# Moving the four query-norm matmuls behind the last attention-value matmuls of each head

## The chip, the cores and the metric

The kernel runs on the 8 cores of one Trainium2 chip. Every core runs the same program on its own batch element (there are 8), and the cores exchange nothing. The metric is the device time of the slowest core in microseconds (us).

## The reference

One transformer layer with its normalizations around each half, per batch element, sequence 2048, width 2048, 16 heads of 128:

```python
# x: [8, 2048, 2048] f32
h   = layernorm(x)
q   = einsum('bpd,hde->bphe', h, W_Q) + b_Q        # k and v likewise
s   = einsum('bqhe,bkhe->bhqk', q, k) / sqrt(128)
s   = where(causal, s, -1e5)
z   = einsum('bkhe,bhqk->bqhe', v, softmax(s))
x   = x + layernorm(einsum('bqhe,hed->bqd', z, W_O) + b_O)
bw  = where(w >= 0, 1, -1) * mean(abs(w), axis=1, keepdims=True)
x   = x + layernorm(einsum('bsi,oi->bso', layernorm(x), bw) + bias)
```

## The kernel before

The program is written as one list of instructions for each engine. `Plan.op` appends an instruction to its engine's list together with the semaphore values that it waits for, so the order of the calls in the Python code is the order on each engine. Nothing reorders them later. Waits are separate small instructions on line 45, one for each semaphore, and each increments or is compared with one counter per engine (PE, DV for VectorE, SC for ScalarE, GP for GpSimd).

Stage A (to about 190 us in the profile) normalizes x, transposes it into `arena_a` (bf16, 16 chunks of 128 features by 2048 positions), and computes q, k and v of head 0 on the way.

Then come the 16 heads, one after the other. For head h, in the order of the code from line 524 on:

- `emit_w_mms(h, 1)` and `emit_w_mms(h, 2)` (line 316) make k and v: 64 matmuls each (line 362), 16 chunks by 4 slices of 512 positions, into four PSUM banks. For k these banks are psD, psE and the two halves of psC; for q and v they are the halves of psA and psB. Four VectorE instructions (line 376) add the bias and write `qt`, `kt`, or v's staging area in `ptil`.
- `emit_mh_sq(which, h)` (line 453) squares q (which = 0) or k (which = 1) with one VectorE instruction of 128x2048 (line 460) into `sqb`, a part of the tile that the profile calls `c`.
- `emit_mh_mms(which, h)` (line 463) multiplies these squares by a matrix of ones: 4 matmuls (line 473) into psA and psB, so that every position's squared norm stands in each row. Each is followed by a VectorE maximum over one row (line 479), and at the end come a maximum of the four (line 485) and a logarithm on ScalarE (line 490). From the norms of q and k comes one number per head, an upper bound of the scores that the exponentials subtract.
- v is transposed (line 554) and copied (line 560). Then four groups g = 0 to 3 of 512 queries follow. Each computes scores (line 572), exponentials on ScalarE (line 586), causal masks on GpSimd (lines 609 and 612), column sums by matmuls with ones (line 622), their reciprocals on ScalarE (lines 627 and 631), the scaling of the probabilities on VectorE (line 641, one instruction for each chunk of 128 keys), the products with v (line 660, 4, 8, 12 and 16 matmuls into psE; called the AV matmuls here), the copy of psE to a staging tile (line 676), and a store to memory (line 679).

PE runs something else while ScalarE and VectorE make the scaled probabilities. In groups 0 to 2 that is the first scores of the next group. In group 3, with no next group, it is the q projection of the next head: lines 650 to 653. This is the place of the change, passed 15 times (after heads 0 to 14), and called a head boundary below:

```python
elif h + 1 < H:
    emit_w_mms(h + 1, 0)      # 64 matmuls, 4 bias adds
    emit_mh_sq(0, h + 1)      # square of q
    emit_mh_mms(0, h + 1)     # 4 matmuls, 5 maxima, 1 logarithm
pe_av = 0
for j in range(chunks):       # 16 AV matmuls in group 3
    wait = [("DV", dv_norm[j])]
```

After the AV matmuls follow the copy of psE (line 676), and then on PE the k projection of head h + 1. Its first matmul writes psD; its waits include the copy of psE, because its second matmul writes psE (lines 339 to 344).

After the heads, the sign weights of the second half are made and transposed (from line 401 on), and 16 row tiles go through the output projection, two normalizations and the second matrix product (lines 718 to 897).

Of the kernel before, what the change touches and what calls it, by code (L numbers as in the profile page):

```python
# [60 lines left out]
def build_program(SEQ, DM, H):  # L61
# [8 lines left out]
    NG = NT // TPG  # L70
# [382 lines left out]
    def emit_mh_sq(which, h):  # L453
        src = (qt_sb, kt_sb)[which]
        if which == 0:
            w0 = [("DV", dv_qkv_evac_d[(h, 0)]), ("PE", pe_mb_prev),
                  ("PE", pe_bw_last), ("PE", pe_norm_last)]
        else:
            w0 = [("DV", dv_qkv_evac_d[(h, 1)]), ("PE", pe_norm_last)]
        dv_sq_d[which] = p.op("vector", lambda e, s=src: e.tensor_mul(  # L460
            sqb, s[:], s[:]), wait=w0, inc="DV")

    def emit_mh_mms(which, h):
        nonlocal pe_norm_last, dv_red_last, sc_lns
        for s in range(NSL):
            hb = s % 4
            wait = [("DV", dv_sq_d[which]), ("CONST", const_t),
                    ("SC", psbuf_last_rd[hb])]
            if which == 1:
                wait.append(("DV", dv_red_d[(0, s)]))  # L470
            if s == 0 and (which == 1 or h == 0):
                wait.append(("DV", dv_qkv_evac_d[(h, 2)]))
            pe_norm_last = p.op("tensor", lambda e, s=s, hb=hb: e.matmul(  # L473
                [psA[:, 0:SLW], psA[:, 512:512 + SLW], psB[:, 0:SLW],
                 psB[:, 512:512 + SLW]][hb], onem_sb[:],
                sqb[:, s * SLW:(s + 1) * SLW], start=True, stop=True),
                wait=wait, inc="PE")
            dv_red_d[(which, s)] = p.op(
                "vector", lambda e, s=s, hb=hb, wh=which: e.reduce_max(
                    srow[0:1, wh * 8 + s:wh * 8 + s + 1],  # L480
                    [psA[0:1, 0:SLW], psA[0:1, 512:512 + SLW],
                     psB[0:1, 0:SLW], psB[0:1, 512:512 + SLW]][hb], AX.X),
                wait=[("PE", pe_norm_last)], inc="DV")
        p.drain("vector")
        dv_mx_d[which] = p.op("vector", lambda e, wh=which: e.reduce_max(  # L485
            srow[0:1, 16 + wh:17 + wh], srow[0:1, wh * 8:wh * 8 + NSL],
            AX.X), inc="DV")
        dv_red_last = dv_mx_d[which]
        p.drain("scalar")
        t_ln = p.op("scalar", lambda e, wh=which: e.activation(  # L490
            srow[0:1, 18 + wh:19 + wh], srow[0:1, 16 + wh:17 + wh], AF.Ln,
            bias=0.0, scale=1.0), wait=[("DV", dv_mx_d[which])],
            inc="SC" if which == 1 else None)
        if which == 1:
            sc_lns = t_ln
# [28 lines left out]
    for h in range(H):  # L524
# [40 lines left out]
        def emit_score(g, j, pe_sc):  # L565
            hb = j % 4
            wait = [("SC", psbuf_last_rd[hb])]
            if j == 0:
                wait += [("DV", dv_vch[h]), ("DV", dv_qkv_all)]
                if g == 0:  # L570
                    wait.append(("DV", dv_mx_d[1]))
            pe_sc[j] = p.op("tensor", lambda e, j=j, g=g, hb=hb: e.matmul(  # L572
                schalf[hb], kt_sb[:, j * 128:(j + 1) * 128],
                qt_sb[:, g * GQ:(g + 1) * GQ], start=True, stop=True),
                wait=wait, inc="PE")
# [27 lines left out]
        for g in range(NG):  # L603
            chunks = (g + 1) * TPG
            gp_mask_j = {}
            for r in range(TPG):
                j = g * TPG + r
                if r > 0:
                    p.op("gpsimd", lambda e, j=j, r=r: e.memset(  # L609
                        ptil[:, j * GQ:j * GQ + r * 128], 0.0),  # L610
                        wait=[("SC", sc_exp[j])], inc="GP")
                gp_mask_j[j] = p.op("gpsimd", lambda e, j=j, r=r: e.tensor_tensor(  # L612
                    ptil[:, j * GQ + r * 128:j * GQ + (r + 1) * 128],
                    ptil[:, j * GQ + r * 128:j * GQ + (r + 1) * 128],
                    tri_sb[:], ALU.mult), wait=[("SC", sc_exp[j])], inc="GP")
            pe_den = 0
            for j in range(chunks):
                wait = [("SC", sc_exp[j])] if j < g * TPG else \
                    [("GP", gp_mask_j[j])]
                if j == 0:  # L620
                    wait.append(("SC", sc_rinv_prev))
                pe_den = p.op("tensor", lambda e, j=j, chunks=chunks: e.matmul(  # L622
                    psC[:, 512:512 + GQ], onem_sb[:], pslot[j],
                    start=(j == 0), stop=(j == chunks - 1)),
                    wait=wait, inc="PE" if j == chunks - 1 else None)
            p.drain("scalar")
            p.op("scalar", lambda e: e.activation(
                psC[:, 512:512 + GQ], psC[:, 512:512 + GQ], AF.Ln,
                bias=0.0, scale=1.0), wait=[("PE", pe_den)])
            p.drain("scalar")  # L630
            sc_rinv = p.op("scalar", lambda e, g=g: e.activation(  # L631
                rbc[g % 2], psC[:, 512:512 + GQ], AF.Exp, bias=0.0, scale=-1.0),
                wait=[("DV", rbc_war[g % 2])], inc="SC",
                lowp="softmax normalizer becomes a bf16 matmul operand")
            sc_rinv_prev = sc_rinv
            dv_norm = {}
            for j in range(chunks):
                wait = [("SC", sc_rinv)] if j == 0 else []
                if j == 0:
                    wait.append(("PE", pe_den))  # L640
                dv_norm[j] = p.op("vector", lambda e, j=j, g=g: e.tensor_tensor(  # L641
                    pslot[j], pslot[j], rbc[g % 2], ALU.mult),
                    wait=wait, inc="DV")
            rbc_war[g % 2] = dv_norm[chunks - 1]
            nchunks = (g + 2) * TPG
            if g + 1 < NG:
                pe_sc = {}
                for j in range(min(4, nchunks)):
                    emit_score(g + 1, j, pe_sc)
            elif h + 1 < H:  # L650
                emit_w_mms(h + 1, 0)
                emit_mh_sq(0, h + 1)
                emit_mh_mms(0, h + 1)
            pe_av = 0
            for j in range(chunks):
                wait = [("DV", dv_norm[j])]
                if j == 0:
                    wait += [("DV", dv_zevac.get(gidx - 1, 0)),
                             ("DV", max(dv_bw_evac_half))]
                pe_av = p.op("tensor", lambda e, j=j, chunks=chunks: e.matmul(  # L660
                    psE[:, 0:GQ], v_sb[:, j * 128:(j + 1) * 128], pslot[j],
                    start=(j == 0), stop=(j == chunks - 1)),
                    wait=wait, inc="PE")
                ptil_slot_av[j] = pe_av
            pe_av_all[h] = pe_av
            if g + 1 < NG:
                sc_exp = {}
                for j0 in range(0, min(4, nchunks), estep):
                    emit_exp(g + 1, j0, pe_sc, sc_exp)
                for j in range(min(4, nchunks), nchunks):  # L670
                    emit_score(g + 1, j, pe_sc)
                    if (j + 1) % estep == 0 and j + 1 > 4:
                        emit_exp(g + 1, j + 1 - estep, pe_sc, sc_exp)
            zpar = gidx % 2
            wait = [("PE", pe_av), (ZWs[zpar], zw_par_t[zpar])]
            dv_zevac[gidx] = p.op("vector", lambda e, zpar=zpar: e.tensor_copy(  # L676
                zstage[zpar], psE[:, 0:GQ]), wait=wait, inc="DV")
            zw_par_t[zpar] = p.op(
                "sync", lambda e, g=g, h=h, zpar=zpar: e.dma_start(
                    zs_h.ap()[g * TPG:(g + 1) * TPG, h].transpose([1, 0, 2]),  # L680
                    zstage[zpar].rearrange("p (t q) -> p t q", q=128)),
                wait=[("DV", dv_zevac[gidx])], inc=ZWs[zpar], incn=16)
            gidx += 1

    B_PE = p.cnt("PE")
    B_DV = p.cnt("DV")
# [253 lines left out]
def _get_nc():  # L940
    key = (_SEQ, _DM, _H)
    if key not in _nc_cache:
        _nc_cache[key] = build_program(*key)
    return _nc_cache[key]
# [30 lines left out]
```

How the kernel before makes its waits and increments, by code:

```python
        def thunk(e, fn=fn, wait=wait, inc=inc, incn=incn, lowp=lowp):  # L43
            for (s, v) in wait:
                e.wait_ge(sems[s][0], v)
            if lowp is not None:
                with nc.allow_low_precision(reason=lowp):
                    ins = fn(e)
            else:
                ins = fn(e)
            if inc is not None:
                ins.then_inc(sems[inc][0], incn)
```

## Time and profile before

| | us |
|---|---|
| runs shown | 2677.37 and 2810.69, median 2744.03 |
| profiled execution, its own time | 2676.51 |
| profiled execution, span of the slowest core (core 7) | 2674.3 |
| spans of the 8 cores | 2662.7 to 2674.3 |
| heads 0 to 15 (about) | 190 to 1855 |
| PE busy on core 7 | 1928.7 (72%) |
| VectorE busy | 992.5 (37%) |
| ScalarE busy | 554.6 (21%) |

The profiled execution is one run, and its rows are those of core 7. A row of the timeline gives the start, the length, the engine, the line of the kernel, output<-input, the shape, and how many instructions stand together; in brackets is how long the engine had been idle before and what released it. A matmul's own length overlaps the next one's, so the distance of starts is what a matmul in a row costs. PE is TensorE, PEld its weight loads, DVE VectorE, ACT ScalarE, POOL GpSimd. PEclk is TensorE's granted clock as a share of full speed, 1.00 being 2.4 GHz and 0.50 being 1.2 GHz.

### The profile page before, as it was taken

Reading aid. Unit: us, or ns where it says so; the run is one execution under the profiler, and the core shown is the slowest. Engines: PE = TensorE matmul, PEld = TensorE weight load, DVE = VectorE, ACT = ScalarE, POOL = GpSimd, SP = SyncE. Lnnn points to the kernel's source line nnn. Section 1 sums busy time; section 2 is a strip of 40 time slices with the busy share of each in tenths; the row PEclk is TensorE's granted clock in tenths of the full one; section 3 lists DMA queues with packets and bytes.
Section 4 is the critical chain, followed back from the end, with each engine's and each line's share of the span. In section 5 each row is a group of like instructions: output and inputs, shape, how many; then the busy total and the mean of one; then the engine's idle time right before and its main releaser. Section 6 shows DMA issues by size and latency. Waiting matters only on the chain.

```text
span 2674.3 us, 27043 instructions; the slowest of 8 cores (2662.7 to 2674.3 us)
## 1 busy us (share of the span) xinstructions
PE 1928.7 (72%) x8180; PEld 827.8 (31%) x8336; DVE 992.5 (37%) x1760; ACT 554.6 (21%) x737; POOL 240.0 (9%) x558
## 2 busy tenths in 40 slices
PE   1457787787777877878778778775438877878874
PEld 1322332332323323323233233232223333333331
DVE  3533333332332232333323333334673435344343
ACT  1223213123032131230321312303001111111110
POOL 1001101011011010110111111201000000000000
PEclk9679898898998988988989889898657988988886
DMA  6322121121221211112113232323322122122110
GB/s 151 110 40 24 12 28 14 20 22 16 25 24 13 28 14 20 22 14 26 22 14 39 35 51 22 46 34 103 112 95 60 53 65 79 40 79 77 42 56 31
DMA packets 178474, 119.32 MB, mean 45 GB/s; under 512 B 168100, under 2 KB 168100, under 8 KB 170148
## 3 DMA queue, kind: packets, MB, share of 16 engines
q0 software_dynamic: 107200, 75.51, 16.8%
q1 hardware_dynamic: 71140, 42.07, 6.3%
q8 instruction: 78, 1.28, 0.2%
q14 instruction: 56, 0.46, 0.1%
HBM read 125.97 MB, written 25.17 MB: 57 GB/s over the span
## 4 chain that ended last, share of the span: by engine, by line
PE 53%; DVE 17%; ACT 10%; issue 9%; DVEq 5%; POOL 3%; DMA 2%; ACTq 1%; POOLq 0%; another core or an unknown queue 0%
PE psA L362 8%; PE psB L362 8%; PE psE L660 7%; ACT ptil L586 5%; PE psC L847 5%; PE psC L362 4%; DVEq L58 4%; PE psC L622 3%; DVE st L210 3%; PE psE L847 2%; PE psD L847 2%; POOL ptil L612 2%; PE psD L362 2%; PE psE L362 2%; DMA c<-x 2%
## 5 line engine op out<-in xcount | busy, mean ns | idle before, releaser
L641 DVE TENSOR_TENSOR ptil<-ptil,c 128x512 bf16<-128x512 bf16 x640 | 220.4, 419 | 482.2 <-ACT c L631 445.4
L362 PE MATMUL psA<-arena_a,wbuf 128*128 128x512 bf16 x1002 | 298.3, 383 | 6.7 <-ACT arena_a L276 3.8
L362 PE MATMUL psB<-arena_a,wbuf 128*128 128x512 bf16 x1002 | 296.5, 380 | 4.9 <-ACT arena_a L276 3.8
L660 PE MATMUL psE<-ptil,v 128*128 128x512 bf16 x625 | 205.4, 428 | 55.8 <-DVE ptil L641 54.7
L622 PE MATMUL psC<-ptil,onem_sb 128*128 128x512 bf16 x624 | 181.6, 403 | 54.0 <-POOL ptil L609 25.0
L586 ACT ACTIVATE ptil<-psA,mbias 128x1024 bf16<-128x1024 f32 x160 | 178.3, 1114 | 183.5 <-PE psE L660 78.4
L847 PE MATMUL psC<-arena_a,c 128*128 128x512 bf16 x496 | 165.8, 416 | 59.5 <-DVE c L834 58.7
L490 ACT ACTIVATE srow<-srow 1x1 f32<-1x1 f32 x32 | 6.5, 202 | 913.6 <-DVE srow L485 913.6
L612 POOL TENSOR_TENSOR ptil<-ptil,tri_sb 128x128 bf16<-128x128 bf16 x256 | 109.2, 426 | 896.2 <-ACT ptil L586 896.1
L586 ACT ACTIVATE ptil<-psB,mbias 128x1024 bf16<-128x1024 f32 x160 | 177.1, 1107 | 0.2 <-PE psB L572 0.2
L572 PE MATMUL psA<-qt,kt 128*128 128x512 bf16 x314 | 107.5, 425 | 81.7 <-ACT ptil L586 51.2
L362 PE MATMUL psC<-arena_a,wbuf 128*128 128x512 bf16 x538 | 155.9, 379 | 4.9 <-DVE qt L376 4.5
L210 DVE BATCH_NORM_STATS2 st<-wbuf 128x6 f32<-128x512 f32 x64 | 39.6, 681 | 317.5 <-ACT wbuf L870 317.5
L362 PEld LDWEIGHTS psA<-arena_a,wbuf 128*128 128x128 bf16 x1024 | 100.8, 99 | 130.0 <-issue 14.3
L362 PEld LDWEIGHTS psB<-arena_a,wbuf 128*128 128x128 bf16 x1024 | 100.3, 98 | 124.0 <-issue 5.6
L660 PEld LDWEIGHTS psE<-ptil,v 128*128 128x128 bf16 x640 | 68.3, 107 | 205.8 <-issue 184.3
L572 PE MATMUL psB<-qt,kt 128*128 128x512 bf16 x315 | 107.9, 427 | 26.1 <-ACT ptil L586 25.7
L473 PE MATMUL psA<-c,onem_sb 128*128 128x512 bf16 x64 | 30.4, 529 | 121.9 <-DVE c L460 76.4
L622 PEld LDWEIGHTS psC<-ptil,onem_sb 128*128 128x128 bf16 x640 | 63.1, 99 | 175.6 <-issue 128.0
L847 PE MATMUL psE<-arena_a,c 128*128 128x512 bf16 x256 | 106.0, 414 | 0.1
L847 PE MATMUL psD<-arena_a,c 128*128 128x512 bf16 x255 | 105.8, 415 | 0.0
L362 PE MATMUL psD<-arena_a,wbuf 128*128 128x512 bf16 x235 | 89.0, 379 | 22.1 <-DVE c L676 21.8
(120 smaller groups left out, 2199.7 us busy)
## 6 DMA issues: line engine op xcount, KB each, us to landing
c<-fw POOLq DMA_DIRECT2D x16, 1024.0 KB, 5.6
ptil<-x SPq DMA_DIRECT2D x16, 1024.0 KB, 7.7
out<-wbuf POOLq DMA_DIRECT2D x16, 1024.0 KB, 5.5
wbuf<-wq POOLq DMA_DIRECT2D x16, 512.0 KB, 8.2
wbuf<-wk POOLq DMA_DIRECT2D x16, 512.0 KB, 7.9
c<-x SPq DMA_DIRECT2D x8, 1024.0 KB, 5.7
wbuf<-wv POOLq DMA_DIRECT2D x16, 512.0 KB, 8.0
zs<-c SPq DMA_DIRECT2D x64, 128.0 KB, 1.9
```

The lines of the kernel that those rows point to most:

```text
L58: self.plans[eng].append(lambda e: e.drain())
L210: p.op("vector", lambda e, g=g, a=src_ap, pr=par: e.bn_stats(st6[pr][:, 6 * g:6 * g + 6], a[:, STW * g:STW * (g + 1)]), wait=w)
L362: e.matmul(banks[bidx], wslot[sl][:, c * 128:(c + 1) * 128], ln1t3[:, c, s * SLW:(s + 1) * SLW], start=(c == 0), stop=(c == NCH - 1)),
L473: pe_norm_last = p.op("tensor", lambda e, s=s, hb=hb: e.matmul([psA[:, 0:SLW], psA[:, 512:512 + SLW], psB[:, 0:SLW], psB[:, 512:512 + SLW] ...
L490: t_ln = p.op("scalar", lambda e, wh=which: e.activation(srow[0:1, 18 + wh:19 + wh], srow[0:1, 16 + wh:17 + wh], AF.Ln, bias=0.0, scale=1. ...
L572: pe_sc[j] = p.op("tensor", lambda e, j=j, g=g, hb=hb: e.matmul(schalf[hb], kt_sb[:, j * 128:(j + 1) * 128], qt_sb[:, g * GQ:(g + 1) * GQ] ...
L586: t_exp = p.op("scalar", lambda e, buf=buf, dst=dst: e.activation(dst, buf, AF.Exp, bias=mbias[:, 0:1], scale=C_ATTN), wait=wait, inc="SC")
L612: gp_mask_j[j] = p.op("gpsimd", lambda e, j=j, r=r: e.tensor_tensor(ptil[:, j * GQ + r * 128:j * GQ + (r + 1) * 128], ptil[:, j * GQ + r * ...
L622: pe_den = p.op("tensor", lambda e, j=j, chunks=chunks: e.matmul(psC[:, 512:512 + GQ], onem_sb[:], pslot[j], start=(j == 0), stop=(j == ch ...
L641: dv_norm[j] = p.op("vector", lambda e, j=j, g=g: e.tensor_tensor(pslot[j], pslot[j], rbc[g % 2], ALU.mult), wait=wait, inc="DV")
L660: pe_av = p.op("tensor", lambda e, j=j, chunks=chunks: e.matmul(psE[:, 0:GQ], v_sb[:, j * 128:(j + 1) * 128], pslot[j], start=(j == 0), st ...
L847: p.op("tensor", lambda e, c=c, s=s: e.matmul(ffnb[s], ln3t[:, c * 128:(c + 1) * 128], bwt3[:, c, s * 512:s * 512 + PSW], start=(c == 0), ...
```

## The change

The call that makes the four norm matmuls of q for the next head moves from ahead of the AV matmuls of group 3 to the end of that group, behind the AV matmuls, the copy of psE and the issue of the store. Its VectorE and ScalarE instructions move with it. The projection and the square stay where they were.

```diff
             elif h + 1 < H:
                 emit_w_mms(h + 1, 0)
                 emit_mh_sq(0, h + 1)
-                emit_mh_mms(0, h + 1)
             pe_av = 0
             for j in range(chunks):
@@
                     zstage[zpar].rearrange("p (t q) -> p t q", q=128)),
                 wait=[("DV", dv_zevac[gidx])], inc=ZWs[zpar], incn=16)
             gidx += 1
+            if g == NG - 1 and h + 1 < H:
+                emit_mh_mms(0, h + 1)
```

No instruction is added or removed. From the AV matmuls on, line numbers are one lower in the changed kernel (660 becomes 659, 676 becomes 675).

On PE, at the first head boundary, with the last two projection matmuls of q (L362 to psA and psB) ahead and the first two of k (to psD and psE) behind; the names in brackets are the counters that each waits for:

```order
 L362 MATMUL psA<-arena_a,wbuf 128x512 x2
 L362 MATMUL psB<-arena_a,wbuf 128x512 x2
+L659 MATMUL psE<-ptil,v 128x512 [waits DV] x16
 L473 MATMUL psA<-c,onem_sb 128x512 [waits DV,CONST,SC] x2
 L473 MATMUL psB<-c,onem_sb 128x512 [waits DV,CONST,SC] x2
-L660 MATMUL psE<-ptil,v 128x512 [waits DV] x16
 L362 MATMUL psD<-arena_a,wbuf 128x512 [waits WS0,DV,SC]
 L362 MATMUL psE<-arena_a,wbuf 128x512 [waits SC]
```

The 16 AV matmuls now stand directly behind the q projection, and the four norm matmuls between them and the k projection.

On VectorE (DVE), at the same boundary before, from the last scaling of the probabilities to the first bias add of k:

```order
L641 TENSOR_TENSOR ptil<-ptil,c 128x512 x16
L376 TENSOR_SCALAR qt<-psA,bqkvT_sb 128x512 x2
L376 TENSOR_SCALAR qt<-psB,bqkvT_sb 128x512 x2
L460 TENSOR_TENSOR c<-qt 128x2048
L479 TENSOR_REDUCE srow<-psA 1x1 x2
L479 TENSOR_REDUCE srow<-psB 1x1 x2
L485 TENSOR_REDUCE srow<-srow 1x1
L676 CAST c<-psE 128x512
L376 TENSOR_SCALAR kt<-psD,bqkvT_sb 128x512
```

And the same stretch of VectorE now:

```order
L641 TENSOR_TENSOR ptil<-ptil,c 128x512 x16
L376 TENSOR_SCALAR qt<-psA,bqkvT_sb 128x512 x2
L376 TENSOR_SCALAR qt<-psB,bqkvT_sb 128x512 x2
L460 TENSOR_TENSOR c<-qt 128x2048
L675 CAST c<-psE 128x512
L479 TENSOR_REDUCE srow<-psA 1x1 x2
L479 TENSOR_REDUCE srow<-psB 1x1 x2
L485 TENSOR_REDUCE srow<-srow 1x1
L376 TENSOR_SCALAR kt<-psD,bqkvT_sb 128x512
```

The copy of psE stands ahead of the five maxima, where it stood behind them. On ScalarE, GpSimd and the store queue the order is the same, since none of them has anything else between the two places.

## Rows read from the trace of the kernel before

**Rows 1.** Spans and granted clock of the cores, slowest core.
```profile
core 7: 2674.3 us, clock 0.862
```

**Rows 2.** Groups of instructions: busy us, mean ns of one | idle before, releasers.
```profile
L660 PE MATMUL psE<-ptil,v 128*128 128x512 bf16 x640 | 209.8, 430 | 52.6 <-DVE ptil L641 52.6
...
L362 PE MATMUL psD<-arena_a,wbuf 128*128 128x512 bf16 x240 | 90.9, 379 | 21.8 <-DVE c L676 21.8
...
L479 DVE TENSOR_REDUCE srow<-psA 1x1 f32<-1x512 f32 x64 | 41.1, 674 | 28.6 <-PE psA L473 28.6
...
L473 PE MATMUL psA<-c,onem_sb 128*128 128x512 bf16 x64 | 30.9, 546 | 121.9 <-DVE c L460 76.3 <-DVE ptil L376 44.7 <-issue 0.2
```

**Rows 3.** Timeline of one head boundary (before head 7), 883 to 908 us.
```profile
883.34 5.46 DVE L641 TENSOR_TENSOR ptil<-ptil,c 128x512 bf16<-128x512 bf16 x16 [9.71 <-ACT c L631]
...
895.27 0.59 PE L362 MATMUL psB<-arena_a,wbuf 128*128 128x512 bf16 x2
895.98 1.41 DVE L376 TENSOR_SCALAR qt<-psA,bqkvT_sb 128x512 bf16<-128x512 f32 x2 [7.18 <-PE psB L362]
...
897.30 1.40 DVE L376 TENSOR_SCALAR qt<-psB,bqkvT_sb 128x512 bf16<-128x512 f32 x2
898.94 1.23 DVE L460 TENSOR_TENSOR c<-qt 128x2048 bf16<-128x2048 bf16 x1 [0.24 <-DVE qt L376]
900.53 1.01 PE L473 MATMUL psA<-c,onem_sb 128*128 128x512 bf16 x2 [4.67 <-DVE c L460]
900.87 0.10 PEld L473 LDWEIGHTS psA<-c,onem_sb 128*128 128x128 bf16 x1 [0.27 <-issue]
901.21 0.10 PEld L473 LDWEIGHTS psB<-c,onem_sb 128*128 128x128 bf16 x1 [0.23 <-issue]
...
902.19 4.26 PE L660 MATMUL psE<-ptil,v 128*128 128x512 bf16 x16
...
903.47 2.49 PEld L660 LDWEIGHTS psE<-ptil,v 128*128 128x128 bf16 x12 [0.28 <-issue]
...
906.63 0.69 DVE L676 CAST c<-psE 128x512 bf16<-128x512 f32 x1 [2.69 <-PE psE L660]
...
907.98 0.38 PE L362 MATMUL psD<-arena_a,wbuf 128*128 128x512 bf16 x1 [1.53 <-DVE c L676]
```

**Rows 4.** Timeline of PE at the first, the longest and the last of 15 boundaries.
```profile
251.73 0.59 PE L362 MATMUL psB<-arena_a,wbuf 128*128 128x512 bf16 x2
...
265.26 0.38 PE L362 MATMUL psD<-arena_a,wbuf 128*128 128x512 bf16 x1 [1.44 <-DVE c L676]
...
1216.53 0.59 PE L362 MATMUL psB<-arena_a,wbuf 128*128 128x512 bf16 x2
...
1230.63 0.38 PE L362 MATMUL psD<-arena_a,wbuf 128*128 128x512 bf16 x1 [1.44 <-DVE c L676]
...
1752.07 0.59 PE L362 MATMUL psB<-arena_a,wbuf 128*128 128x512 bf16 x2
...
1764.69 0.38 PE L362 MATMUL psD<-arena_a,wbuf 128*128 128x512 bf16 x1 [1.47 <-DVE c L676]
```

**Rows 5.** Stretches: us, busy (instructions) of PE, PEld, DVE, ACT, POOL, PEclk, DMA share, GB/s.
```profile
872.80:878.00 5.20, 2.88 (x12) 0.96 (x10) 0.69 (x1) 4.59 (x5) 0.00 (x0) 1.00 0.13 30
892.00:895.40 3.40, 3.40 (x17) 1.57 (x16) 0.00 (x0) 0.00 (x0) 0.00 (x0) 1.00 0.00 0
900.10:903.40 3.30, 2.87 (x7) 1.01 (x8) 2.25 (x5) 0.00 (x0) 0.00 (x0) 0.50 1.06 105
908.00:934.00 26.00, 26.00 (x121) 11.89 (x122) 3.95 (x5) 0.00 (x0) 1.14 (x1) 1.00 0.24 26
1904.00:1916.00 12.00, 10.16 (x50) 4.40 (x48) 2.26 (x3) 2.02 (x2) 0.00 (x0) 0.81 0.25 87
```

**Rows 6.** Timeline of PE in the output projection, clock 0.81.
```profile
1904.33 0.70 PE L744 MATMUL psA<-arena_b,qt 128*128 128x512 bf16 x2
1904.86 0.70 PE L744 MATMUL psB<-arena_b,qt 128*128 128x512 bf16 x2
```

## The prediction

> **What bounds the kernel now.** I read the spans first: the eight cores lie within half a per cent of each other, core 7 being the slowest with 2674.3 us at a mean granted clock of 0.862 [rows 1]. Its program took 2676.51 us in the profiled execution, 2.2 us more than the span; this is the execution that my sum starts from. The two runs shown are 2677.37 and 2810.69 us, so the sum stands beside the lower one and 67 us under their median of 2744.03.
>
> Then I read the groups for what PE waits for around the moved step. The norm matmuls (L473) had PE idle for 76.3 us with the square on VectorE (L460) as the releaser, and the first matmul of the k projection (L362 to psD) had it idle for 21.8 us until psE was copied out (L676) [rows 2]. Both stand at the head boundaries.
>
> Then the timeline of one boundary [rows 3]. The last matmul of the q projection starts at about 895.49. (A pair starts at 895.27, and starts are 0.22 us apart.) VectorE cannot begin the four bias adds of q before the projection is done; it runs them from 895.98, squares q from 898.94 to 900.17, and only then can PE start a norm matmul, at 900.53, after 4.67 us without work. The 16 AV matmuls stand behind these four on PE and start at 902.19, although their operands were ready at 888.80, when the last scaling (L641) ended. The copy of psE runs from 906.63 to 907.32, and the k projection starts at 907.98. Nothing else is at work that the end could depend on: VectorE, ScalarE and GpSimd all wait for PE. So the boundary is one serial chain, and a microsecond taken out of it comes off the span.
>
> From the last start of the q projection to the first of the k projection this boundary takes 907.98 - 895.49 = 12.49 us. The first of the fifteen takes 265.26 - 251.95 = 13.31 the longest 1230.63 - 1216.75 = 13.88, and the last 1764.69 - 1752.29 = 12.40 [rows 4]. All fifteen lie between the last two, and their mean is 13.17.
>
> Last, the clock [rows 5]. It is 1.00 through the q projection, falls to 0.50 behind the idle 4.67 us, and is back at 1.00 for the k projection. How long it stays low is most of what makes the boundaries differ.
>
> **What the change does, step by step.** It removes and adds no instruction. It reorders PE and VectorE at 15 places.
>
> (a) The AV matmuls start directly behind the q projection. Sixteen matmuls at full clock cost 0.22 us each: the twelve weight loads in a row at the end of the AV block span 2.49 us, so starts are (2.49 - 0.10) / 11 = 0.217 apart [rows 3]. That is 3.5 us, from about 895.9 to 899.4. They run beside VectorE's bias adds and square, which take PE's start from 895.49 to 900.53, that is 5.04 us, before and after alike. The AV block fits inside, with some 1.2 us over. It costs nothing there. Were the cover gone (AV at half clock throughout, 16 x 0.43 = 6.8 us) it would stand out by about 2.2 us a boundary.
>
> (b) The four norm matmuls still start at +5.04 us, since the square's time is unchanged. Each carries three waits, which PE's sequencer works off one by one, and this sets their distance: the weight loads at 900.87 and 901.21 are 0.34 us apart, with a matmul's own share at full clock being 0.22 [rows 3]. So 3 x 0.34 = 1.0 us to the last of them.
>
> (c) The first matmul of the k projection comes next, with six waits of its own. From the end of the copy of psE (907.32) to its start PE spent 0.66 us on the last four or five of them [rows 3], so six take about 0.7 to 0.8. That puts it at +5.04 + 1.0 + 0.8 = +6.8 us. It could be as little as +6.4, were the waits worked off behind running matmuls.
>
> (d) Is the copy of psE late now? On VectorE it follows the square, so it starts at +4.75 (900.24), AV having ended just before, and ends at +5.4. The k projection wants it at about +6.1. So the wait that cost 1.4 to 1.5 us in each of rows 3 and 4 is hidden behind the norm matmuls, with 0.6 us to spare.
>
> (e) The four maxima (0.67 us each [rows 2]) and the rest of the step fall beside the k projection. That takes 128 matmuls together with v, of which the first 64 run 13.8 us before VectorE has its next bias add to do. 4 x 0.67 + 0.15 = 2.8 us is hidden with a wide margin. v's projection, which writes psA and psB again, comes 13.8 us later and does not wait for them.
>
> Sum: 13.17 - 6.8 = 6.4 us a boundary, times 15 = 96 us. 2676.5 - 96 = 2580.5; I take 2581. With +6.4 in place of +6.8 it is 102 us (2575).
>
> The bounds. (b) and (c) have 0.4 us either way, that is 6 us. Further on in each head the clock falls a second time, behind v's projection, and how the rest of a head falls against the clock's changes may shift by half a microsecond a head in either direction: 8 us. Together the forecast's own range is 2568 to 2596.
>
> **Rivals.**
>
> *The clock falls at the boundary all the same.* Against it: 1.2 us without work is far less than the 4.67 that preceded the fall, and between 872.80 and 878.00 PE had 2.88 busy of 5.20 us in short pieces and the clock stayed at 1.00 [rows 5]. For it: no boundary in this trace shows so short a gap, and the four norm matmuls behind it are spaced widely. Price: the norm matmuls go to 0.43 apart (+0.3 us), and the k projection starts at half clock. The longest low stretches at a boundary (13.9 against 12.4 us of boundary time) allow about 2.5 us lost there. That is up to 2.8 x 15 = 42 us, so 2623; the usual case is near 2610.
>
> *The denser stretch brings the clock down: slower than before.* The q projection, AV, norms and the projections of k and v now form one almost unbroken block: 64 + 16 + 4 + 128 = 212 matmuls, where so far at most 128 stood together. In the output projection the same program falls to 0.81 in a dense stretch (1904 to 1916), and there two matmuls take 0.53 us [rows 5, 6], so 0.263 each in place of 0.217: 0.046 more. If that level held in the whole block and in the 16 column sums ahead of it, it would cost 228 x 0.046 = 10.5 us a head, 157 us in 15 heads, and the time would be 2581 + 157 = 2738, slower by 2.3%. The place is the k and v projections; it decides from the point where the level holds for about 9 of every 15 of these matmuls, since there the 96 us are used up. Against it: the 26 us of the k and v projections from 908 to 934, with PE busy throughout, ran at 1.00, with the other seven cores at the same program [rows 5].
> The Trainium skill ("TensorE: Matmul & The Clock Gate", section "Seeing it yourself") says that a peak-current limit takes a whole die to 13/16 of the clock once three of its cores run dense matmuls. By that rule alone, heads would have run at 0.81 already. The trace does not agree in the heads (1.00 from 908 to 934) and does agree in the output projection.
>
> *Nothing is gained.* If AV could not start behind the q projection, because one of its waits ended as late as the square's, the order would not matter: AV would go from +5 us, and the time would stay within 1% of 2676, the small gain being the copy of psE. Against it: its operands come from L641, finished 7 us earlier [rows 3], and its other two waits are for the copy of group 2, long past, and for work that has not begun in the heads.
>
> **How the numbers follow.** The forecast 2581: 0.79. The clock falls anyway, 2610 to 2623: 0.11. The 0.81 level, 2738: 0.05. Nothing gained, about 2665: 0.05. About 2% (2623) is what a measurement of this kernel can tell from no change. The forecast lies wholly beyond it, and the clock rival nearly wholly; 0.02 of that one I put within. So faster 0.88, same 0.07, slower 0.05. The range: 2566 to 2640 takes in the forecast's own range and the clock rival with a little over, and leaves out 0.1.
>
> **What would show it.** Right, if in the changed profile the distance from the last q matmul to the first k matmul is about 6.8 us at all fifteen boundaries, with the norm matmuls at +5.0 behind about 1.2 us of idleness; if PE's idle time before L473 put down to the square falls from 76.3 to about 25 us and that before L362 to psD, 21.8 us, vanishes; and if the stretch behind AV shows 1.00. The mean granted clock should rise from 0.862, to about 0.88. The AV step is wrong if AV starts later than +0.6 us; the norm step if L473 starts are further apart than 0.34; the copy step if L362 to psD still names the copy of psE as its releaser; the clock step if the first us of the k projection stand at 0.50. The whole is wrong if the heads take as long as before, or if stretches at 0.81 show up in them.

## The result, and the profile after

The changed kernel takes 2579.85 us (median of 11 runs) against 2676.93 (median of 10 runs of the kernel before). The ratio is 0.9637, with a 95% interval from 0.9621 to 0.9653: faster by 3.6%. The profiled execution took 2576.0 us, 100.5 less than the 2676.5 from which the sum started. The ratio and the verdicts below leave out executions in which the cores of one die, or of both, showed a lower mean granted clock (down to 0.75 to 0.84 in those of the changed kernel, against 0.87 to 0.88) and which took longer, and of which no trace was kept; without them the median of the changed kernel is 2576.6 us, which is the level of 2576 that the experiments below are compared with.

First, how much of this lies in the heads. The matmul that spreads a head's score offset (L515) runs once in each head, so its first and last start mark off fifteen heads. The first view gives span and mean granted clock of core 3 (now the slowest) and of core 7 (the one that was shown before); the second gives, for that line and the same two cores, the durations and the first and last start.

```profile
core 3: 2573.4 us, clock 0.876
...
core 7: 2568.5 us, clock 0.877
```

```profile
L515 PE MATMUL psC<-nm_bf,oner_sb x16: 179/179/182, 196.8 to 1708.7; 1*128 1x1 bf16 x16
...
L515 PE MATMUL psC<-nm_bf,oner_sb x16: 179/179/181, 193.9 to 1704.1; 1*128 1x1 bf16 x16
```

On core 7 the heads take 1704.1 - 193.9 = 1510.2 us. The same line of the kernel before ran there from 197.3 to 1803.3, which is 1606.0. That is 95.8 us less; over all eight cores the mean is 95.5. Behind the last head core 7 needs 2568.5 - 1704.1 = 864.4 us in place of 2674.3 - 1803.3 = 871.0. This second difference is none of the change's: in the execution profiled before, the cores 4 to 7 ran about 72 us of the second half at a clock of 0.81 (the stretch in [rows 5]), and the four others did not and took 862 to 865 us there. The same place of core 7 is now at 0.99:

```profile
1805.00:1815.00 10.00, 7.37 (x46) 3.44 (x43) 2.97 (x3) 2.02 (x2) 0.00 (x0) 0.99 0.14 57
```

The groups that answer to [rows 2], now those of core 3:

```profile
L659 PE MATMUL psE<-ptil,v 128*128 128x512 bf16 x640 | 188.5, 390 | 51.4 <-DVE ptil L641 51.4
...
L362 PE MATMUL psD<-arena_a,wbuf 128*128 128x512 bf16 x240 | 91.4, 381 | 4.5 <-issue 3.2 <-DVE srow L479 1.3
...
L473 PE MATMUL psA<-c,onem_sb 128*128 128x512 bf16 x64 | 25.8, 430 | 69.9 <-DVE ptil L376 44.7 <-DVE c L460 24.4
```

PE's idle time before the norm matmuls that is put down to the square fell from 76.3 to 24.4 us. What is left of the wait for the copy of psE is nothing: the 21.8 us before the k projection are 4.5, and none of it names L675. The 44.7 us of the norm matmuls of k are as before; the change does not touch them. An AV matmul's mean went from 430 to 390 ns, since the clock no longer falls ahead of it: at the boundaries the starts of AV were 0.309 us apart and are 0.217 apart now, on the mean of all cores.

The timeline of the first boundary on core 3, to be held beside [rows 3]:

```profile
251.51 0.59 PE L362 MATMUL psB<-arena_a,wbuf 128*128 128x512 bf16 x2
...
251.95 3.62 PE L659 MATMUL psE<-ptil,v 128*128 128x512 bf16 x16
252.22 1.41 DVE L376 TENSOR_SCALAR qt<-psA,bqkvT_sb 128x512 bf16<-128x512 f32 x2 [7.14 <-PE psB L362]
...
255.19 1.23 DVE L460 TENSOR_TENSOR c<-qt 128x2048 bf16<-128x2048 bf16 x1 [0.24 <-PE psE L659]
256.33 0.68 DVE L675 CAST c<-psE 128x512 bf16<-128x512 f32 x1
...
256.77 0.74 PE L473 MATMUL psA<-c,onem_sb 128*128 128x512 bf16 x2 [1.21 <-DVE c L460]
...
257.25 1.28 DVE L479 TENSOR_REDUCE srow<-psA 1x1 f32<-1x512 f32 x2 [0.24 <-PE psA L473]
...
258.47 0.38 PE L362 MATMUL psD<-arena_a,wbuf 128*128 128x512 bf16 x1 [0.28 <-issue]
```

The last q matmul starts at 251.73. AV follows at +0.22, the norm matmuls at +5.04 behind 1.21 us of idleness, and the k projection at 258.47 - 251.73 = +6.74. The copy of psE lies beside the end of that. Over the fifteen boundaries of this core the distance is 6.78 us on average (it was 13.17 on core 7), and at the one shown the clock stays at its upper level throughout:

```profile
251.00:254.00 3.00, 3.00 (x16) 1.37 (x14) 1.78 (x3) 0.00 (x0) 0.93 (x1) 1.00 0.00 0
254.40:256.00 1.60, 1.16 (x6) 0.31 (x4) 1.36 (x2) 0.00 (x0) 0.00 (x0) 1.00 0.69 57
256.00:258.00 2.00, 1.23 (x4) 0.38 (x4) 1.76 (x4) 0.00 (x0) 0.00 (x0) 1.00 1.67 163
258.00:284.00 26.00, 25.72 (x120) 11.68 (x120) 5.82 (x9) 0.20 (x1) 1.14 (x1) 1.00 0.28 30
```

### The profile page after: what moved, and what is told of

Its sections match the earlier page's. It is cut to its first block, busy times and chain, and to the rows that moved or that the text cites. A ratio compares the mean times of both kernels' runs of the same rounds, so it can differ in the third digit from the quotient of the medians.

```text
span 2573.4 us, 27199 instructions; the slowest of 8 cores (2564.2 to 2573.4 us)
## 1 busy us (share of the span) xinstructions
PE 1915.6 (74%) x8336; PEld 820.4 (32%) x8336; DVE 990.5 (38%) x1760; ACT 554.5 (22%) x737; POOL 239.3 (9%) x558
## 4 chain that ended last, share of the span: by engine, by line
PE 53%; DVE 17%; ACT 10%; issue 9%; DVEq 4%; POOL 4%; DMA 2%; ACTq 1%; POOLq 0%
PE psA L362 9%; PE psB L362 9%; PE psE L659 7%; ACT ptil L586 5%; PE psC L848 5%; PE psC L362 5%; DVEq L58 4%; DVE st L210 3%; PE psC L622 3%; PE psD L848 2%; PE psE L848 2%; POOL ptil L612 2%; PE psD L362 2%; PE psE L362 2%; DMA c<-x 2%
## 5 line engine op out<-in xcount | busy, mean ns | idle before, releaser
L362 PE MATMUL psA<-arena_a,wbuf 128*128 128x512 bf16 x1024 | 304.4, 384 | 5.0 <-ACT arena_a L276 3.1
L362 PE MATMUL psB<-arena_a,wbuf 128*128 128x512 bf16 x1024 | 303.5, 383 | 3.2 <-ACT arena_a L276 3.2
L659 PE MATMUL psE<-ptil,v 128*128 128x512 bf16 x640 | 188.5, 390 | 51.4 <-DVE ptil L641 51.4
L362 PE MATMUL psC<-arena_a,wbuf 128*128 128x512 bf16 x544 | 158.1, 381 | 4.5 <-DVE qt L376 4.5
L362 PEld LDWEIGHTS psA<-arena_a,wbuf 128*128 128x128 bf16 x1024 | 101.0, 99 | 131.1 <-issue 16.4
L362 PEld LDWEIGHTS psB<-arena_a,wbuf 128*128 128x128 bf16 x1024 | 100.8, 99 | 125.4 <-issue 8.5
L659 PEld LDWEIGHTS psE<-ptil,v 128*128 128x128 bf16 x640 | 62.3, 97 | 187.7 <-issue 152.9
L221 ACT ACTIVATE rstd<-mv,epsb_sb 128x1 f32<-128x1 f32 x64 | 18.9, 296 | 405.2 <-DVE mv L213 285.5
L362 PE MATMUL psD<-arena_a,wbuf 128*128 128x512 bf16 x240 | 91.4, 381 | 4.5 <-issue 3.2
```

The source lines that it names most:

```text
L221: p.op("scalar", lambda e, pr=par: e.activation(rstd[pr][:], mv2[pr][:, 1:2], AF.Ln, bias=epsb_sb[:, 0:1], scale=1.0), wait=w)
L362: e.matmul(banks[bidx], wslot[sl][:, c * 128:(c + 1) * 128], ln1t3[:, c, s * SLW:(s + 1) * SLW], start=(c == 0), stop=(c == NCH - 1)),
```

## The experiments

For each I give one more number, read from the granted clock and the matmul starts of all eight cores: the time from the first q matmul of a boundary to the last v matmul behind it (a block), averaged over 8 x 15 = 120 boundaries, and in how many of them the clock fell to 0.50 inside. Before the change a block takes 54.12 us and the clock falls in 120 of 120; after it, 47.86 us and 6 of 120. The difference, 6.26 x 15 = 94 us, is nearly all of the 95.5 us that the heads became shorter. The two need not agree so well: what is saved in a block can be given back in part in the rest of the head, so I give the change of the heads (first to last L515, mean of the cores) too where it differs.

**Only VectorE's order undone.** The norm matmuls stay behind AV; their maxima stand ahead of the copy of psE again.

```diff
+            if g == NG - 1 and h + 1 < H:
+                emit_mh_mms(0, h + 1)
             wait = [("PE", pe_av), (ZWs[zpar], zw_par_t[zpar])]
@@
-            if g == NG - 1 and h + 1 < H:
-                emit_mh_mms(0, h + 1)
```

> The order on PE is that of the changed kernel; on VectorE the five maxima stand ahead of the copy of psE again, as before the change. The theory of the hidden copy: the norm matmuls start 5.04 us behind the last q matmul as in the changed kernel, the four maxima (0.67 us each) run from +5.7 to +8.4, then the one of the four and the drain, the copy from about +8.6 to +9.3, and the k projection starts at +9.9 to +10.0 in place of +6.8. That is 3.2 us x 15 = 48 us over the changed kernel's fast level of 2576, about 2624. PE is then without work for some 3.5 us, so by the theory that a long idle stretch brings the clock down the first microseconds of the k projection run at 1.2 GHz, for 1 to 2 us more a boundary: 2640 to 2650. If the place of the copy does not matter (rival), the time is that of the changed kernel, 2576, and the k projection starts at +6.8.

Measured: 2650.18 us, ratio 0.992 (0.9903 to 0.9938), the upper end of the 2640 to 2650 that the theory of the copy together with the clock gave. The timeline of the first boundary (core 1), and the clock in two stretches:

```profile
250.46 0.59 PE L362 MATMUL psB<-arena_a,wbuf 128*128 128x512 bf16 x2
...
255.72 0.74 PE L473 MATMUL psA<-c,onem_sb 128*128 128x512 bf16 x2 [1.21 <-DVE c L460]
...
257.41 1.27 DVE L479 TENSOR_REDUCE srow<-psB 1x1 f32<-1x512 f32 x2
258.76 0.14 DVE L485 TENSOR_REDUCE srow<-srow 1x1 f32<-1x4 f32 x1
258.94 0.69 DVE L677 CAST c<-psE 128x512 bf16<-128x512 f32 x1
...
260.20 0.59 PE L362 MATMUL psD<-arena_a,wbuf 128*128 128x512 bf16 x1 [3.06 <-DVE c L677]
```

```profile
260.20:265.60 5.40, 5.40 (x13) 1.94 (x14) 0.00 (x0) 0.00 (x0) 0.00 (x0) 0.50 0.10 24
266.00:290.00 24.00, 24.00 (x113) 10.89 (x112) 3.95 (x5) 0.00 (x0) 1.14 (x1) 1.00 0.24 22
```

The k projection starts 9.52 us behind the last q matmul (250.68), where the expectation had 9.9, and its first 13 matmuls run at half clock. A block takes 52.81 us, with a fall in 120 of 120. So, with PE in its new order, where the copy stands on VectorE is worth 74 of the 94 us (75 of the heads' 95.5): 2.8 us a boundary directly (the distance is 9.56 us on average against 6.78), and 2.2 us by what the longer gap does to the clock, which stands at 0.50 for 6.7 us of a block against 0.2 in the changed kernel. The order on PE alone gives only 20. It shortens the distance by 3.6 us, but the idle stretch has moved to the place ahead of the k projection, 3.1 us long, and the low clock now slows that projection. The copy's place under PE's old order was not tried, so the two shares hold for this order of steps only.

**The old order, with the idle time filled.** Twenty matmuls that nobody reads are added in the old gap.

```diff
                 emit_mh_sq(0, h + 1)
+                for _ in range(20):
+                    p.op("tensor", lambda e: e.matmul(
+                        psD[:, 0:512], onem_sb[:], ln1t3[:, 0, 0:512],
+                        start=True, stop=True))
                 emit_mh_mms(0, h + 1)
```

> The kernel before, in its old order, with 20 extra matmuls of 128x512 into psD (which nobody reads) between the q projection and the norm matmuls of the next head. They take 20 x 0.217 = 4.3 us and lie in the 4.67 us in which PE waits for the square. This holds the clock up and changes nothing else, so it separates the clock's part of the gain from the order's. Theory (clock 1.5 us and order 4.9 us a boundary): the distance from the last q matmul to the first k matmul falls from 13.2 to about 11.6 us (5.04 to the norms, 1.3 for them, 3.5 for AV, 0.6 and 0.7 for the copy, 0.65 for the waits), the time by 1.5 x 15 = 23 us, to about 2648 to 2652, and no fall of the clock stands at a boundary. Rival (the clock is most of it): over 50 us gained. Rival (the clock falls at this place anyway, on a schedule of its own): 2671, as before, with 0.50 at the boundary.

Measured: 2649.33 us, ratio 0.9919 (0.9899 to 0.9938). The first boundary (core 6) and its clock:

```profile
250.61 4.48 PE L654 MATMUL psD<-arena_a,onem_sb 128*128 128x512 bf16 x20
...
255.44 0.71 PE L473 MATMUL psA<-c,onem_sb 128*128 128x512 bf16 x2 [0.35 <-DVE c L460]
...
261.76 0.38 PE L362 MATMUL psD<-arena_a,wbuf 128*128 128x512 bf16 x1 [1.44 <-DVE c L680]
```

```profile
250.00:261.00 11.00, 9.98 (x44) 4.06 (x42) 7.07 (x11) 0.20 (x1) 1.16 (x1) 1.00 0.50 48
```

The distance is 261.76 - 250.40 = 11.36 us, a block takes 52.39, and the clock fell in none of the 120, though PE still idles 1.45 us ahead of the k projection. The heads are 22.9 us shorter than before the change, as expected (23). So keeping the clock up is worth 1.7 us a boundary in the old order, and the rest of the 6.3 is the order itself: AV beside VectorE's work and the copy beside the norms. It also disposes of a clock that falls at this place on a schedule of its own: with the idle 4.67 us filled (0.35 of them are left), and nothing else changed, it does not fall.

**A second square.** The square of q is done twice in the changed kernel, which lengthens VectorE's chain.

```diff
                 emit_mh_sq(0, h + 1)
+                p.drain("vector")
+                emit_mh_sq(0, h + 1)
```

> The changed kernel with the square of q done twice at each boundary, which makes VectorE's chain 1.23 us and a drain longer. Theory (VectorE's bias adds and square set where the norm matmuls start, AV being hidden beside them): they start at +6.3 to +6.5 in place of +5.04, the k projection at +8.1, and the time rises by 1.3 to 1.4 us x 15 = 20 us to about 2596. PE's idle stretch behind AV grows from 1.2 to 2.5 us; if a stretch of that length brings the clock down, about 1 to 1.5 us a boundary come on top: 2610 to 2620. Rival (PE's own work sets the boundary): no change, 2576.

Measured: 2606.93 us, ratio 0.9755 (0.9736 to 0.9775); against the 2576 of the changed kernel 31 us more, where 20 were expected without a fall of the clock and 34 to 44 with one. The first boundary (core 6), and the clock behind it:

```profile
253.82 1.23 DVE L460 TENSOR_TENSOR c<-qt 128x2048 bf16<-128x2048 bf16 x1 [0.30 <-DVE c L460]
...
255.43 0.71 PE L473 MATMUL psA<-c,onem_sb 128*128 128x512 bf16 x2 [2.76 <-DVE c L460]
```

```profile
257.00:260.20 3.20, 3.07 (x8) 1.25 (x9) 1.53 (x4) 0.20 (x1) 0.00 (x0) 0.50 0.07 16
```

The norm matmuls start at 255.43 - 248.84 = +6.59 and the k projection at +8.29, so the VectorE chain does set the boundary. PE's gap grew to 2.76 us here (2.84 on average), and the clock now falls in 114 of 120 blocks (50.21 us each). Of the 2.35 us that a block grew, 1.6 are the longer distance and some 0.7 the clock.

**One wait in place of twelve.** The norm matmuls of q keep the wait for the square on the first of them; the others are implied by what PE and VectorE have done before.

```diff
+            if which == 0 and h > 0:
+                wait = [("DV", dv_sq_d[0])] if s == 0 else []
```

> The changed kernel, with the semaphore waits of the four norm matmuls of q (from head 1 on) cut from three each to one on the first of them; the others are implied by what PE and VectorE have done before. Theory (PE's sequencer works the waits off one by one, and this spaces the norm matmuls 0.34 us apart): their distance becomes 0.22 us, the norm matmuls still start at +4.8 to +5.0, and the k projection at about +6.2 in place of +6.8; 0.4 to 0.6 us x 15 = 6 to 9 us less than the changed kernel's fast level of 2576, so 2567 to 2570. Rival (the waits are worked off behind running matmuls and cost nothing): 2576.

Measured: 2564.98 us, ratio 0.9606 (0.9592 to 0.962), 11 us under the changed kernel, where 6 to 9 were expected; a block takes 46.87 us, the clock falls in none, and the heads are 10.4 us shorter. The first boundary on core 2:

```profile
256.90 0.59 PE L475 MATMUL psA<-c,onem_sb 128*128 128x512 bf16 x2 [1.00 <-DVE c L460]
257.33 0.59 PE L475 MATMUL psB<-c,onem_sb 128*128 128x512 bf16 x2
...
257.96 0.38 PE L362 MATMUL psD<-arena_a,wbuf 128*128 128x512 bf16 x1
```

The norm matmuls are 0.22 us apart (two in 0.43), they start at +4.82, since two waits fewer stand between the square's end and the first of them, and the k projection starts at +5.88. That is 0.9 us less than in the changed kernel (5.87 against 6.78 on average), where I had expected 0.4 to 0.6. The trace has each wait as an instruction of its own on line 45, 0.106 us after the one before it. Of the 0.9, 0.2 are the earlier start, 0.4 the closer spacing, and 0.3 lie behind the last norm matmul: the six waits of the k projection, untouched by the edit, begin at 257.83 in the changed kernel, just after the last norm matmul has started (257.81), and here five of them begin at 257.40, before it has (257.55). That last part I had not counted.

**The norms moved further, into the k projection.**

```diff
-            emit_w_mms(h, 1)
+            emit_w_mms(h, 1, at=8, hook=lambda: emit_mh_mms(0, h))
@@
-            if g == NG - 1 and h + 1 < H:
-                emit_mh_mms(0, h + 1)
```

Here and below, `hook` is called inside the projection's loop ahead of chunk `at`.

> The changed kernel with the four norm matmuls of q and their maxima moved on once more, from ahead of the k projection to behind its first 8 chunks. AV stays behind the q projection. Theory: the copy of psE, which ends 5.3 us behind the last q matmul, is now what the k projection waits for; it starts at about +5.95 in place of +6.8, and the norm matmuls cost 0.9 to 1.1 us inside it, since PE's queue of running matmuls covers their waits. So last q matmul to last v matmul goes from 34.2 to between 34.2 and 34.5 us, and the time stays within 5 us of 2576. PE idles 1.9 to 2.0 us in one piece ahead of the k projection, more than the 1.2 of the changed kernel and less than the 2.8 of the run with a second square, where the clock fell; if it falls here too, 1 to 1.5 us a boundary come on top: 2590 to 2600.

Measured: 2596.8 and 2597.3 us in the two executions that the ratio of 0.9725 (0.9704 to 0.9746) rests on (the median of all five is 2621.6): the case with a fall of the clock. The first boundary on core 4:

```profile
255.43 0.69 DVE L677 CAST c<-psE 128x512 bf16<-128x512 f32 x1
...
256.68 0.38 PE L364 MATMUL psD<-arena_a,wbuf 128*128 128x512 bf16 x1 [2.02 <-DVE c L677]
```

```profile
257.30:260.50 3.20, 3.20 (x9) 1.14 (x8) 0.00 (x0) 0.00 (x0) 0.00 (x0) 0.50 0.46 67
```

The k projection starts earlier, at +5.85, and yet a block takes 49.29 us, 1.4 longer than in the changed kernel. Behind an idle stretch of 2.02 us the clock falls in 110 of 120 blocks. The norm matmuls, which take 1.0 us on PE, were doing a second job where the change had put them: they cut the gap, into 1.21 us ahead of them and 0.28 us behind.

**AV inside the q projection, norms inside the k projection.** The AV matmuls and the copy stand behind the first 12 chunks of the q projection.

```diff
-                emit_w_mms(h + 1, 0)
+                emit_w_mms(h + 1, 0, at=12, hook=lambda: emit_copy(emit_av()))
@@
-            emit_w_mms(h, 1)
+            emit_w_mms(h, 1, at=8, hook=lambda: emit_mh_mms(0, h))
```

> A further step on from the changed kernel: the 16 AV matmuls and the copy of psE stand inside the q projection (behind the first 12 of its 16 chunks), and the four norm matmuls with their maxima inside the k projection (behind its first 8 chunks). Neither VectorE's bias adds and square nor the copy is then waited for. If those waits are all that is left at the boundary: from the first q matmul to the last k matmul the changed kernel takes 13.6 + 6.8 + 13.6 = 34.0 us; now 144 matmuls x 0.216 = 31.1, the norms 1.0 to 1.3 and the waits ahead of the k projection 0.2 to 0.7, so 32.4 to 33.1; 0.9 to 1.6 us x 15 = 14 to 24 us less, 2552 to 2562. Rival (the denser block brings the clock to 0.81, or something else in the head takes over): 2576 or more.

Measured: 2613.77 us, ratio 0.9785 (0.9768 to 0.9802), 37 us over the changed kernel where 14 to 24 less were expected. A miss. The timeline (core 4, with the last q matmul at 255.41) shows what I had overlooked:

```profile
257.23 1.40 DVE L378 TENSOR_SCALAR qt<-psB,bqkvT_sb 128x512 bf16<-128x512 f32 x2
258.87 1.23 DVE L462 TENSOR_TENSOR c<-qt 128x2048 bf16<-128x2048 bf16 x1 [0.24 <-DVE qt L378]
258.88 0.59 PE L364 MATMUL psD<-arena_a,wbuf 128*128 128x512 bf16 x1 [3.09 <-DVE qt L378]
```

The k projection waits for the bias adds of q (line 344). In the changed kernel they are over when PE comes to that wait, because AV and the norms stand between. Without that cover PE idles for 3.09 us, and the clock falls in 118 of 120 blocks.

**The same without that wait.** The k projection writes other banks than the q projection, and what it does not need was left out from head 1 on.

```diff
-                                 ("DV", dv_qkv_evac_d.get((h, 0), dv_bank_free))]
+                        if h == 0 or only_slice is not None:
+                            wait.append(("DV", dv_qkv_evac_d.get(
+                                (h, 0), dv_bank_free)))
```

> The run with AV inside the q projection again, without the one wait that I overlooked there: the first matmul of the k projection waits for the four bias adds of q (line 344), which in the changed kernel are over by then, and which kept PE idle for about 4 us once the AV matmuls no longer stood behind the q projection. The k projection writes other banks (psD, psE, psC), so from head 1 on the wait is left out. Theory (that wait and the fall of the clock behind it were the whole miss): no gap between the q and the k projection, no fall at the boundary, from the first q matmul to the last matmul of the k projection 32.4 to 33.1 us against 34.0, and 2552 to 2562. Rival (something else, such as the copy of psE or the denser block): it stays near 2614, or above 2576.

Measured: 2546.01 us, ratio 0.9531 (0.9516 to 0.9546). The first boundary (core 1) and its clock:

```profile
251.24 0.59 PE L366 MATMUL psA<-arena_a,wbuf 128*128 128x512 bf16 x2
251.58 0.69 DVE L675 CAST c<-psE 128x512 bf16<-128x512 f32 x1 [7.19 <-PE psE L662]
...
254.69 0.38 PE L366 MATMUL psD<-arena_a,wbuf 128*128 128x512 bf16 x1
...
261.60 0.59 PE L477 MATMUL psA<-c,onem_sb 128*128 128x512 bf16 x2
262.03 0.59 PE L477 MATMUL psB<-c,onem_sb 128*128 128x512 bf16 x2
```

```profile
238.00:283.00 45.00, 45.00 (x211) 20.38 (x208) 16.67 (x32) 0.84 (x3) 2.30 (x2) 1.00 0.38 39
```

PE is busy for 45 us without a gap, all 120 blocks take 45.54 us, and 212 matmuls x 0.215 = 45.6. From the first q matmul to the last of k it is 31.72 us, where 32.4 to 33.1 were expected. The heads are 29.6 us shorter than in the changed kernel, less than the 35 us of the blocks. The time beats my expectation by 6 us at the least, because the waits cost nothing inside a dense stretch: the norm matmuls keep their three waits each and still start 0.22 us apart, as do the first matmuls of the k projection.

**The norms of k inside the v projection too.** They write psD, psE and psC there.

```diff
-            emit_w_mms(h, 2)
+            emit_w_mms(h, 2, at=8, hook=lambda: emit_mh_mms(1, h))
```

> As the run before it, and the same cure applied to the norm matmuls of k: they stand inside the v projection (behind its first 8 chunks) and write psD, psE and psC in place of psA and psB. Behind the v projection only the bias adds of v are left ahead of the transposes of v. Theory: the transposes start 3.4 us behind the last v matmul in place of 6.9, the norm matmuls cost 0.9 us inside, so 2.6 us x 15 = 39 us less than the run before it, about 2518; the clock still falls behind the v projection, since PE idles for 3 us there, which leaves 20 us either way. Rival (the exponentials' offset mbias, at the end of the same chain of small steps, is late by as much as is gained): within 10 us of the run before it.

Measured: 2497.15 us, ratio 0.9348 (0.9331 to 0.9364), 49 us under the kernel of the experiment before it, where 39 with 20 either way were expected. The transposes of v start 3.48 us behind the last v matmul (285.22) on core 7:

```profile
285.01 0.59 PE L366 MATMUL psB<-arena_a,wbuf 128*128 128x512 bf16 x2
...
288.70 1.86 PE L566 MATMUL psA<-eye_sb,ptil 128*128 128x128 bf16 x16 [3.09 <-DVE ptil L380]
```

Over all 120 boundaries that wait is 3.47 us in place of 6.85, and a block is 0.86 us longer by the four norm matmuls, so 2.5 us a head or 38 us are accounted for. The heads became 48 us shorter. The other 10 go together with the clock, which stood at 0.50 for 256 us of the heads in the run before this one and stands there for 172 now (mean of the cores); which of the shorter waits brought that about was not tested. This version beats both kernels, by 6.5% and by 3%.

## Why the prediction was right, step by step

**The sum.** 6.4 us a boundary and 96 us in all were predicted; the heads became 95.8 us shorter on core 7 and 95.5 on the mean of the cores. The distance at the boundaries gives 6.34 x 15 = 95 of it, so the rest of the heads, for which the prediction allowed 8 us either way, hardly shifted. The profiled execution fell to 2576.0 and not to the 2580.5 of the sum. Most of the difference is the stretch at 0.81 behind the heads, which was in the execution that the sum started from and is no part of the change. The ratio predicted (2580.5 / 2676.5 = 0.964) lies inside the measured interval.

**(a) AV costs nothing where it goes.** Right: it runs from +0.22, beside the bias adds and the square, and the norm matmuls still start at +5.04.

**(b) and (c) Norms and waits, +6.8.** Right in sum, 6.78 measured, from two small errors that cancel: the norm matmuls stand 0.353 us apart on average where 0.34 was said (1.06 us in place of 1.0), and the six waits behind the last of them take 0.67 us where 0.7 to 0.8 was said. By the prediction's own sign the norm step is wrong beyond 0.34; it is so by 0.013 us. The run with one wait shows that this part is really the waits: without eleven of them 0.9 us more are gained.

**(d) The copy of psE is not late.** Right, and worth more than the prediction told. It started at +4.6 rather than +4.75. The prediction counted its hiding as 1.4 to 1.5 us a boundary; with VectorE's order undone the boundary lost 2.8 us directly and nearly 5 with the clock, 74 us in all. Before, the copy waited for AV and not for the maxima; with AV moved ahead, it is the maxima that would hold it up.

**(e) The maxima are hidden.** Right: no row of the k projection waits for them to any amount that counts (1.3 us in total before L362 to psD).

**The clock.** Right for 114 of 120 boundaries: no fall behind an idle stretch of 1.2 us. The sum did not say how much of its 6.4 us is the clock; the run with the idle time filled puts that at 1.7 in the old order. In the six others the rival came true, for up to 1.8 us each (the longest block is 49.62 us against 47.86 on average). The mean granted clock was forecast at about 0.88 and is 0.877 on core 7.

**The rivals.** The 0.81 level does not show in the heads, not even with 45 us of matmuls in one piece (the run with AV inside the q projection and without the wait for the bias adds). The Trainium skill ("TensorE: Matmul & The Clock Gate", section "Seeing it yourself") has dense matmuls on three or more cores of a die bring 13/16 of the clock; in the profiled executions the heads do not bear that out, and the output projection did so on the four cores of one die before and on none after.

## What to carry to other kernels

In a serial chain between two engines, place independent work of the waiting engine exactly behind the instruction whose result the other engine has to process, and look at the other engine's queue as well: 74 of the 94 us hang on the copy of psE standing ahead of five small maxima on VectorE. Before moving work out of a gap, list every wait of the instruction behind it. One that is satisfied today only because of the cover (the bias adds of q) becomes the new gap. And waits are only free behind work: the same three of them cost 0.14 us a matmul behind an idle stretch (0.353 us apart) and nothing inside a dense one (0.216).

## What the runs showed of the hardware that was not expected

The clock reacts to gaps much shorter than the 4.67 us of the kernel before. Behind the dense q projection and AV, an idle stretch of 1.2 us was followed by a fall to 0.50 at 6 of 120 boundaries, one of 2.0 us at 110, one of 2.8 us at 114, and one of 3.1 us at 118 in one run and at 120 in another. It fell at none of 120 in the run with one wait (1.0 us idle, and the norm matmuls behind it 0.22 us apart), and at none in the run with the idle time filled, although 1.45 us without work stand ahead of its k projection. So the length of one idle stretch does not decide it alone, and what else does was not tested. The Trainium skill ("TensorE: Matmul & The Clock Gate", section "Why this matters for your kernels") advises to avoid idle gaps of PE above about 3 us between bursts. These runs differ from it: 2.0 us was followed by a fall nearly every time, and that cost 20 us in the run that had its norms inside the k projection.
